# Totals of nodes that cross a tile border: from a row carried between tiles to a PSUM accumulator of its own

## The reference

```python
# layer 0
h = relu(concat(x[src], edge_attr) @ W1 + b1) @ W2 + b2
agg = segment_sum(h, dst) / maximum(count, 1)
out = relu(concat(x, agg) @ W3 + b3) @ W4 + b4
# layer 1
e = exp(e - max over dst);  out[dst] += (x @ W.T)[src] * e / sum over dst of e
# layer 2
out = relu(segment_sum(norm * (x @ W.T + b)[row], col))      # self loops included
# layer 3
h = segment_sum((x @ W_gcn)[src] * weight, dst) + b_gcn
out = h @ W_fc.T + b_fc
```

## Time and profile before

| | us |
|---|---|
| median of 3 runs | 3378.82 |
| lowest, highest | 3373.29, 3382.97 |
| span of the profiled execution | 3386.8 |

### The profile page before, as it was taken

How to read it: one execution, slowest core, us unless ns; L and a number is a source line. 1 busy time by engine, 2 the same in 40 slices (tenths; PEclk the granted TensorE clock), 3 DMA queues, 4 the chain that set the end, 5 groups by cost and what they waited for, 6 DMA issues and landing times. The chain is left out here.

```text
span 3386.8 us, 41659 instructions
## 1 busy us (share of the span) xinstructions
PE 2409.5 (71%) x13104; PEld 2063.8 (61%) x13104; DVE 1788.8 (53%) x3382; ACT 1223.3 (36%) x2110; POOL 1006.1 (30%) x839
## 2 busy tenths in 40 slices
PE   6779999999969999999979849200005969966600
PEld 6779888888859888888867736100003557754400
DVE  4523232323334544455446565699974579955522
ACT  2133233333333333233335533333324545534421
POOL 0000000000012332233133313566553067752065
PEclk9889999999979999999979965555555589988855
DMA  5101101010224232422243302343434255543388
GB/s 173 37 14 49 37 32 41 27 41 23 41 90 140 87 100 98 140 95 91 81 137 88 85 15 84 121 152 126 139 114 145 82 175 178 179 148 113 112 286 269
DMA packets 189198, 354.10 MB, mean 105 GB/s; under 512 B 28605, under 2 KB 41917, under 8 KB 189097
## 3 DMA queue, kind: packets, MB, share of 16 engines
q1 hardware_dynamic: 129536, 239.71, 20.4%
q0 software_dynamic: 42880, 91.15, 9.7%
q10 hardware_dynamic: 16688, 21.99, 1.9%
HBM read 279.42 MB, written 128.16 MB: 120 GB/s over the span
## 5 line engine op out<-in xcount | busy, mean ns | idle before, releaser
L1848 PE MATMUL f_s_ps<-f_Yh,f_match 128*128 128x258 f32 x80 | 40.1, 501 | 415.3 <-issue 414.7
L1848 PEld LDWEIGHTS f_s_ps<-f_Yh,f_match 128*128 128x128 f32 x80 | 24.7, 309 | 442.0 <-issue 438.0
L132 PE MATMUL b_y_ps<-W23h,b_Rh 128*128 128x320 f32 x800 | 249.1, 311 | 0.0
L470 POOL DMA_INDIRECT b_X<-in_x,b_idx x48 | 48.4, 1008 | 669.3 <-PE b_tp_ps L659 655.4
L133 PE MATMUL b_y_ps<-W23l,b_Rh 128*128 128x320 f32 x800 | 246.2, 308 | 0.5 <-issue 0.5
L134 PE MATMUL b_y_ps<-W23h,b_Rl 128*128 128x320 f32 x800 | 246.1, 308 | 0.3
L132 PE MATMUL b_hid_ps<-b_hTh,W1h 128*128 128x512 f32 x500 | 202.9, 406 | 13.2 <-issue 13.2
L132 PE MATMUL c_u_ps<-c_W3h,c_hTh 128*128 128x320 f32 x640 | 202.0, 316 | 0.0
L133 PE MATMUL b_hid_ps<-b_hTl,W1h 128*128 128x512 f32 x500 | 201.4, 403 | 0.0
L134 PE MATMUL b_hid_ps<-b_hTh,W1l 128*128 128x512 f32 x500 | 201.1, 402 | 0.0
L591 DVE TENSOR_TENSOR b_Rl<-b_R,b_Rh 128x512 fp32r<-128x512 f32 x100 | 69.3, 693 | 248.6 <-ACT b_Rh L524 248.6
(11 more groups left out here) (326 smaller groups left out, 7505.5 us busy)
## 6 DMA issues: line engine op xcount, KB each, us to landing
c_X<-in_x SPq DMA_DIRECT2D x21, 1024.0 KB
x<-n_O SPq DMA_DIRECT2D x20, 1032.0 KB, 4.7
g_X<-x SPq DMA_DIRECT2D x20, 1032.0 KB
x<-c_XB SPq DMA_DIRECT2D x20, 1024.0 KB, 4.7
n_X<-x SPq DMA_DIRECT2D x20, 1024.0 KB, 8.9
x<-g_O SPq DMA_DIRECT2D x20, 1024.0 KB
i_X<-x SPq DMA_DIRECT2D x20, 1024.0 KB
c_XB<-in_x SPq DMA_DIRECT2D x19, 1024.0 KB
```

The costliest lines, as they stand in the source:

```text
L132: pe.matmul(out, ah, bh, start=first, stop=False)
L470: pool.indirect_dma_start(X[:, i // GROUP, i % GROUP, :], None, a["x"][:, :], bass.IndirectOffsetOnAxis(idx[:, i:i + 1], 0), bounds_check= ...
L1848: pe.matmul(s[:, 2 * j + h, 0:HW], match[:, b, j, :], Yh[:, j, w], start=True, stop=False)
```

## The change

No row goes from tile to tile any more. Row 0 of a tile, which was free for the carry, has weight zero. A node whose edges span a border gets its total in a second accumulator: PSUM tile `c`, of 40 rows, where row k belongs to the node with which tile k begins. `heads` (128 x 40 for each tile) holds a one where an edge's destination is that node, and each tile adds `heads(t)^T @ Y(t)` to `c`, which is opened and closed with matmuls of zeros. At the end of the stage the 40 rows are scaled or copied as a tile is and stored as rows 5120 to 5159 of the table; a new index `slot2` sends the nodes concerned there. The node stages use `slot2`, with the same number of gathers.

- `layer1_sums`, `layer2_edges`: four bulk matmuls and four into `c`; L1494, L1853 and ACT's copies of row 0 are gone. PSUM holds the sums of two tiles (`RS = 2`) where it held four. PE's loops are written out, 40 tiles long. In layer 2 the copy to `T` is shared: DVE the first half of the columns, ACT the second.
- `match` of all 40 tiles is built once, by DVE, in `layer1_softmax` ahead of the comparison of `ids`, and stays up to layer 3.
- `layer3_edges`: the `nx` matmuls, ACT's row copies and the building of `match` are gone; one matmul a tile into `cT`; behind the last group a high and a low part of `cT`, one product with `W_fc` and one more store.
- `layer1_messages`: `Wraw` and `Wrow` share memory with the second buffer of `X`, so the second group's gathers wait until both have been read.
- `prepare`: one more index load, five more DVE steps, a second `val2`; `hist` is multiplied with 160 columns in one of its two products (80 before), and DVE makes two products of 320 elements a block where it made one.

```diff
@@ prepare
+                step(dve.tensor_tensor(at_head[:, :], dst_i[:, :], keep["heads"][:, :], ALU.is_equal))
+                step(dve.tensor_tensor(move[:, :], first_i[:, :], slot_i[:, :], ALU.subtract))
+                step(dve.tensor_tensor(move[:, :], move[:, :], at_head[:, :], ALU.mult))
+                step(dve.tensor_tensor(move[:, :], move[:, :], slot_i[:, :], ALU.add))
+                step(dve.tensor_tensor(val2[:, :], last[:, :], move[:, :], ALU.mult))
...
+                step(dve.memset(keep["wgt"][0:1, :], 0.0))
...
+                        mm = pe.matmul(hist[:, 1, 0:2 * NT], onehot[:, 2, j, :], rowed[:, j, :], start=False, stop=False)
@@ layer1_messages
-        Wraw = sb("Wraw", [P, KF, F])
-        Wrow = sb("Wrow", [P, KF, F])
+        Wraw, Wrow = X[:, 1, 0, :, :], X[:, 1, 1, :, :]
...
                 gather(0, 0, 0, 0)
+                pool.wait_ge(w_lo, 1)
+                pool.wait_ge(proj_ready, 1)
@@ new
+def head_matrix(dve, keep, heads):
+
+    return dve.tensor_tensor(heads[:, :, :], over(keep["heads"][:, :].unsqueeze(1), [P, ET, ET]),
+                             over(keep["dst"][:, 0:ET].unsqueeze(2), [P, ET, ET]), ALU.is_equal)
@@ layer1_softmax
+                for g in range(EG):
+                    w = slice(g * GROUP, (g + 1) * GROUP)
+                    dve.tensor_tensor(match[:, w, :], keep["rows"][:, g * (GROUP * P):(g + 1) * (GROUP * P)].rearrange("p (j q) -> p j q", q=P),
+                                      over(keep["dst"][:, w].unsqueeze(2), [P, GROUP, P]), ALU.is_equal).then_inc(built, 1)
@@ layer1_sums
+    RS = 2
...
-                    for j in range(GROUP):
-                        for h in range(2):
-                            act.wait_ge(sum_ready, g * (2 * GROUP) + (2 * j + h + 1))
-                            act.copy(carry[0:1, h, 0:LW[h]], s[0:1, 2 * j + h, 0:LW[h]]).then_inc(carry_ready, 1)
...
+                dve.memset(zeros[:, :], 0.0).then_inc(init, 1)
+                head_matrix(dve, keep, heads).then_inc(init, 1)
...
-                    dve.wait_ge(carry_ready, t * 2 + 3)
+                    dve.wait_ge(sum_ready, t + 1)
...
+                normed(T[0:ET, 0, :], c[0:ET, :, :], ET, ET)
...
+                for g in range(EG):
+                    for j in range(GROUP):
+                        t = g * GROUP + j
+                        pe.wait_ge(y_lo, t + (1 + GROUP))
+                        pe.wait_ge(scaled, t + 1)
+                        own = match[:, t, :]
+                        head = heads[:, t, :]
+                        for h in range(2):
+                            w = slice(GW * h, GW * h + LW[h])
+                            pe.matmul(s[:, 2 * (j % RS) + h, 0:LW[h]], own, Yh[:, j, w], start=True, stop=False)
+                            mm = pe.matmul(s[:, 2 * (j % RS) + h, 0:LW[h]], own, Yl[:, j, w], start=False, stop=True)
+                        mm.then_inc(sum_ready, 1)
+                        for h in range(2):
+                            w = slice(GW * h, GW * h + LW[h])
+                            pe.matmul(c[0:ET, h, 0:LW[h]], head, Yh[:, j, w], start=False, stop=False)
+                            mm = pe.matmul(c[0:ET, h, 0:LW[h]], head, Yl[:, j, w], start=False, stop=False)
+                        mm.then_inc(row_ready, 1)
@@ layer2_edges
+                def out(r, i):
+                    j = i % GROUP
+                    act.wait_ge(sum_ready, r * GT + (i + 1))
+                    act.wait_ge(stored[j], r * 32 + 16 * (i // GROUP))
+                    act.copy(T[:, j, HW:W], s[:, 2 * (i % RS) + 1, 0:HW]).then_inc(t_out[1], 1)
...
-                        dve.tensor_copy(T[:, j, :].rearrange("p (a f) -> p a f", a=2), s[:, 2 * j:2 * j + 2, 0:HW]).then_inc(out_ready, 1)
+                        dve.tensor_copy(T[:, j, 0:HW], s[:, 2 * (i % RS), 0:HW]).then_inc(t_out[0], 1)
@@ layer3_edges
-                        pe.matmul(nx[0:1, 0:D], match[:, b, j, 0:1], Y[:, j, :], start=True, stop=True).then_inc(next_ready, 1)
...
+                        mm = pe.matmul(sT[:, j * P:(j + 1) * P], Y[:, j, :], own, start=True, stop=True)
                         if j == GROUP - 1:
                             mm.then_inc(sum_ready, 1)
+                        mm = pe.matmul(cT[:, 0:ET], Y[:, j, :], head, start=False, stop=False)
```

More of the change, by code:

```diff
@@ L36 @@
 ROWS_N = NT * P
+ROWS_T = ROWS_E + ET
 EPS = 1e-5
@@ L1457, in group @@
+                    normed(T[:, j, :], s[:, 2 * (j % RS):2 * (j % RS) + 2, :], t, P)
+                def group(g, last):
                     for j in range(GROUP):
-                        if not (last and j >= 2):
+                        if j < GROUP - 2:
                             split(g, j + 2)
+                        elif not last:
+                            split(g + 1, j + 2 - GROUP)
                         sums(g, j)
-                build_match(0, 0)
                 split(0, 0)
@@ L1464, in _ @@
                 split(0, 1)
[L1465 to L1469 removed]
+                with dve.Fori(0, EG - 1) as g:
+                    group(g, False)
+                group(EG - 1, True)
+                dve.wait_ge(row_ready, ET + GROUP + 1)
+                dve.wait_ge(stored[0], 16 * EG)
+                normed(T[0:ET, 0, :], c[0:ET, :, :], ET, ET)
@@ L1499, in layer1_nodes @@
+                for h in range(2):
+                    mm = pe.matmul(c[0:ET, h, 0:LW[h]], zeros[:, 0:ET], zeros[:, 0:LW[h]], start=False, stop=True)
+                mm.then_inc(row_ready, 1)
 def layer1_nodes(nc, core, a, keep, x1, T1, x2):
@@ L1689, in layer2_edges @@
     ln_step, var_ready, std_ready, norm_ready, h_ready = (sem("f_" + n) for n in ("lnstep", "var", "std", "norm", "h"))
-    init, masked, carry_ready, match_ready, sum_ready, out_ready = (
-        sem("f_" + n) for n in ("init", "masked", "carry", "match", "sum", "out"))
-    y_hi, y_lo, bulk_ready = sem("f_yhi"), sem("f_ylo"), sem("f_bulk")
+    init, masked, y_hi, y_lo, sum_ready, row_ready = (sem("f_" + n) for n in ("init", "masked", "yhi", "ylo", "sum", "row"))
+    t_out = [sem("f_o0"), sem("f_o1")]
     stored = [sem(f"f_st{b}") for b in range(GROUP)]
+    RS = 2
     GT = 2 * GROUP
@@ L1839, in _ @@
+                pe.sem_inc(t_out[1], RS)
+                pe.sem_inc(row_ready, GROUP)
+                pe.wait_ge(init, 2)
+                for h in range(2):
+                    pe.matmul(c[0:ET, h, 0:HW], zeros[:, 0:ET], zeros[:, :], start=True, stop=False)
+                for r in range(ER):
                     for i in range(GT):
-                        j, b = i % GROUP, i // GROUP
+                        j, b = i % GROUP, i % RS
                         t = r * GT + i
-                        if j == 0:
-                            pe.wait_ge(match_ready, r * 2 + (b + 1))
@@ L1844, in _ @@
                         pe.wait_ge(y_lo, t + 1)
-                        pe.wait_ge(out_ready, t + 1)
+                        for h in range(2):
+                            pe.wait_ge(t_out[h], t + 1)
+                        own = match[:, t, :]
+                        head = heads[:, t, :]
                         for h in range(2):
                             w = slice(HW * h, HW * h + HW)
-                            pe.matmul(s[:, 2 * j + h, 0:HW], match[:, b, j, :], Yh[:, j, w], start=True, stop=False)
-                            mm = pe.matmul(s[:, 2 * j + h, 0:HW], match[:, b, j, :], Yl[:, j, w], start=False, stop=False)
@@ L1858, in layer2_nodes @@
+                        mm.then_inc(row_ready, 1)
+                for h in range(2):
+                    mm = pe.matmul(c[0:ET, h, 0:HW], zeros[:, 0:ET], zeros[:, :], start=False, stop=True)
+                mm.then_inc(row_ready, 1)
 def layer2_nodes(nc, core, a, keep, x2, T2, x3):
@@ L2146, in layer3_edges @@
     tp_ready, tp_free, hT_hi = sem("h_tp"), sem("h_tpfree"), sem("h_hThi")
-    m_ready, m_out, y_ready, y_out, match_ready = sem("h_m"), sem("h_mout"), sem("h_y"), sem("h_yout"), sem("h_match")
-    row_ready, next_ready, carry_ready, sum_ready = (sem("h_" + n) for n in ("row", "next", "carry", "sum"))
+    m_ready, m_out, y_ready, y_out = sem("h_m"), sem("h_mout"), sem("h_y"), sem("h_yout")
+    y_read = sem("h_yread")
+    sum_ready, rows_done, row_hi, row_lo = (sem("h_" + n) for n in ("sum", "rows", "rowhi", "rowlo"))
     sum_hi, sum_lo, z_ready, z_out = sem("h_sumhi"), sem("h_sumlo"), sem("h_z"), sem("h_zout")
```

330 lines of the change are left out of this document (151 added, 179 removed).

## The result

| | before | after |
|---|---|---|
| median, us | 3380.89 (4 runs, 3373.29 to 3383.71) | 3272.22 (4 runs, 3259.57 to 3286.98) |
| ratio | | 0.969, 95% interval 0.966 to 0.972 |
| span of the profiled execution | 3386.8 | 3266.1 |

The account below looks back on a forecast made before the run. The carry passes were taken to set the pace of layers 1 and 2. Terms +2.3 + 9 + 1.7 - 46.4 - 29.7 + 0.5 = -62.6 took 3378.8 to 3316 us, range 3284 to 3350.

Parts of the forecast that it names:

- 2.0 a tile: `layer1_sums`: the period falls from 3.19 to 2.0 us a tile, bounds 1.75 and 2.6, gain 46.4.
- 88.5 us for layer 2: `layer2_edges` after the PE wait: 29.3 x 2.46 + 15.6 + 0.8 = 88.5 in place of 118.2, so -29.7.
- the hold: `layer2_edges`: 23 us in which PE does one tile while POOL's gathers are on their way; taken as unchanged.
- some 0.1 a group: `layer3_edges`: removing `nx`, ACT's row copies and `match` gives only some 0.1 a group, 1.0 in all; stage taken as +0.5.
- What bounds the kernel: `layer1_sums` and `layer2_edges`: the carry sets the pace, 2.0 of the 3.19 us a tile in layer 1.
- Rival 1: `layer1_sums`: each `Yl` waits for POOL's multiply at the shared port, 2.6 a tile, gain 22, total 3340; chance 0.22.
- 8 x 1.95: `layer2_edges`, last round, without statistics or normalised rows: eight tiles at 1.95, 15.6 us.
- The extra tail: End of `layer3_edges`: a copy, a subtraction, three passes, an addition and a store waiting for one another, 2.2 us.
- 2 (the hold hangs on the carry): `layer2_edges`: PE's 23 us wait is tied to the carry and goes too, gain another 20, total 3296; chance 0.11.
- 3 (the ring of two sums): `layer2_edges`: PE needs DVE and ACT for every tile; 2.85 a tile, gain 12 not 30, total 3334; chance 0.12.
- 4 (instruction loading): PE's written-out loops must be brought from DRAM, six pieces of 25.7, 154 us, total 3470; chance 0.05 with milder forms.
- layer 1's lower bound: `layer1_sums`: DVE alone at 1.75 a tile, gain up to 56; counted as 12 more in the range's lower end.

Follow-up runs that it names:

- the first pair: Profiles of the kernel before and the changed kernel, the first taken: span 3386.8 against 3266.1, `layer3_edges` 173.5 against 165.0.
- nonx: Kernel before with paced gathers, in layer 3 without `nx` matmuls, ACT's copies of row 0 and the carry: `layer3_edges` 140.2, against 154.0 with them.
- the pair on one chip: Kernel before and changed kernel, both unpaced, profiled on the same chip: `layer2_edges` 175.4 against 131.4, `layer3_edges` 172.7 against 168.4.

## Why the prediction was wrong

The six stages that the change touches were forecast at -62.6 and gave -102.0. Of the 39.4 that were missing, 12.5 are in `layer1_sums`, 13.8 in `layer2_edges`, 9.0 in `layer3_edges` and 4.4 in `layer1_messages`. The steps that failed are the terms of three stages: 2.0 a tile, 88.5 us for layer 2 behind the hold, and "some 0.1 a group" in layer 3.

- **What bounds the kernel.** Right: the carry passes were the pace of layers 1 and 2, and without them the tile is bound by other engines.
- **layer1_sums.** The mechanism was right, the term 2.0 a tile was mis-sized; it is 1.65, and 40 x 0.35 = 14 covers the 12.5 that were missing. I had put the two limits where they are, but added up the wrong things. For the port I took both of POOL's instructions and `Yl`, 1.97; the small copy doesn't add to it, since it ends together with the `Yl` that it waits for. For DVE I took 1.85 from durations and 1.75 for their overlap, where start to start gives 1.65. Rival 1 (2.6 a tile) had the right port, but took the stretched rows of the stage's first tiles for the steady state; there `Yl` takes 0.69. The clock went to the higher level, which I hadn't weighed: a tile's eight matmuls take 1.20 of PE there (2046.39 to 2047.59), where I had 1.7 to 2.2, which would have been a bound above 1.65.
- **layer2_edges.** The hold stayed, with its length, as taken; it ended 57.0 us into the stage, 58.0 before. What came behind it took 75.6 and not 88.5. The steady rate was mis-sized: a round took 18.0 (2550.05 to 2568.04 between the same statistics) and not 19.7, since a DVE tile took 2.12 and an ACT tile 2.20, not 2.24 and 2.4. And the last round was priced at 8 x 1.95, for which the prediction shows no rows, where the records show 0.94 from one `Yl` to the next and 1.1 on the mean of five such steps; the granted clock there is 0.81, again mostly the higher level:

```profile
2588.04 0.69 DVE L1820 TENSOR_TENSOR f_Yl<-f_X,f_Yh 128x516 fp32r<-128x516 f32 x1
2588.64 0.42 DVE L1836 COPY f_T<-f_s_ps 128x258 f32<-128x258 f32 x1
2588.98 0.69 DVE L1820 TENSOR_TENSOR f_Yl<-f_X,f_Yh 128x516 fp32r<-128x516 f32 x1
```

  That is about 6 for the 29.3 tiles, about 7 in the last round and 1 in the hold: the 13.8 that were missing.
- **layer3_edges.** The step that failed is "gives only some 0.1 a group": it is 0.38 (11.53 to 11.15), and putting the build of `match` back takes 0.31 of it. In the first pair seven groups give 2.7, the first 0.5 and the last 0.8. The extra tail cost what I had put it at (10.1 behind the last weighting, where nonx, which has neither, took 7.6: 2.5), but the missing round trips of the last group gave back 2 of it (9.7 to 7.6) and not 0.5. The other 5.0 of the 8.5 lie ahead of the first weighting, where the hold is, and are luck: in the pair on one chip the whole stage gave 4.3. Which part of the gain is `nx` and which is `match` stays open beside gathers.
- **layer1_messages, layer1_softmax, prepare.** Right in kind and size: +4.6 to 8 for a forecast of 9, +1.4 for 1.7, +1 to 3 for 2.3. In `layer1_messages` the shared memory is the cause, shown by taking it away.
- **Rivals.** 2 (the hold hangs on the carry) is refuted by the same pacing in both kernels: 19.4 and 20.9. 3 (the ring of two sums) did not come: 2.2 a tile. 4 (instruction loading) left no mark, in `layer1_sums`, which has no gathers, the longest wait of PE between tiles is 1.3 us, and it is for DVE. The port's rival is above.
- **The range.** It had room for one stage that gives more, and three gave more at once, two of them since I priced steps by the durations of records taken at a pace set by something else. With the measured stages the sum is -102.0 in the first pair and -98.6 in the pair on one chip, so 3277 to 3280; the remaining distance to 3272 is within the scatter of the node stages. Two sums were off by a little: layer 1's lower bound gives 10 and not 12 (56 - 46.4), and the chances of the forecast, the rivals and no change add up to 1.02.

## What to carry to other kernels

When the bound goes away, price the new period from start to start of back-to-back instructions on the next engine, and write the limits as alternatives: here DVE's list gave 1.65 and the shared port 1.61, and taking away one of them gave next to nothing. A stretch in which an engine finishes and nobody notices is worth an experiment of its own: holding POOL's gathers back to the pace of their use cost one wait and gave 21 to 22 us in layer 2 on chips with the hold, a fifth of the whole change. Where an experiment takes work from PE, read the granted clock beside its time: here it fell from 0.93 to 0.50 and the run lost most of its meaning. And compare such stretches on more than one chip before explaining them by the kernel.

## What was not expected of the hardware

- On chips with the hold, four of six, PE's semaphore increments were seen late, by up to 23 us in the rows read (2497.2 to 2520.3), while POOL's indirect gathers ran one behind the other (1.3 us each), on ACT and DVE alike; increments of DVE that PE waits for were not. Plain loads of the same size by SP had no such effect. With 18 gathers ahead and then one a tile layer 2 showed nothing of it; layer 3 did. What in the chip delays them is open, as is why two chips don't.
- The granted clock of `layer1_sums` went from 0.50, with PE busy for 95% of the time, two thirds of it carry passes over one partition, to 0.93 with PE busy for 70%. With the matmuls into `c` left out as well it was 0.50 again, with PE busy for 69%. What sets the level isn't shown.
